# A decoder layer on one core: a new order for all five attention queues, and the gate product read from PSUM

## What is computed

```python
x = x + cross_attention(layernorm(x), ctx, mask)      # 16 heads of 16, rotary, softmax over 256 keys
x = x + gated_linear_attention(layernorm(x))          # 16 heads, decayed state, per-head norm,
                                                      # silu(inputs @ Wg + bg) * o @ Wo
x = x + ffn(layernorm(x))                             # shared expert + top 2 of 7 routed experts
```

## Time and profile before

| | before |
|---|---|
| median of 3 runs | 1606.47 us (1604.30 to 1606.73) |
| the profiled execution, its own time | 1609.45 us |
| its span, first to last instruction | 1607.6 us |
| TensorE busy, whole span | 1451.6 us (90%) |
| VectorE, ScalarE, GpSimd busy | 1097.7, 855.7, 775.0 us |
| chain that ended last, by engine | TensorE 56%, VectorE 23%, ScalarE 11%, DMA 4% |
| first product of keys | at 30.21 us |
| first product of the experts | at 939.15 us |

### The profile page before, as it was taken

One profiled execution on the slowest core, in us unless ns is written; L12 is line 12 of the kernel. 1 busy time (PEld: TensorE's weight loads), 2 busy tenths in 40 slices (PEclk: granted clock), 3 DMA queues, 4 the chain that ended last, 5 costly groups with the idle time before them and its releaser, 6 DMA issues.

```text
span 1607.6 us, 43463 instructions
## 1 busy us (share of the span) xinstructions
PE 1451.6 (90%) x17222; PEld 1090.2 (68%) x17222; DVE 1097.7 (68%) x1975; ACT 855.7 (53%) x1850; POOL 775.0 (48%) x689
## 2 busy tenths in 40 slices
PE   3788998999999999999998766999999999999987
PEld 2455665666666766666666555878888888888865
DVE  2786889888888888888888469774444444444457
ACT  1566876777778777777777322452323222222321
POOL 1575777767676767776776300003333333333210
PEclk9898999999999999999999678999999999999998
DMA  5577776777777776767784332643322222222182
GB/s 135 110 161 132 141 135 129 138 143 130 144 129 148 137 149 135 147 129 139 128 154 84 70 99 73 172 138 67 70 69 73 70 71 70 73 71 72 50 265 73
DMA packets 468338, 185.98 MB, mean 116 GB/s; under 512 B 418065, under 2 KB 456289, under 8 KB 468145
## 3 DMA queue, kind: packets, MB, share of 16 engines
q1 hardware_dynamic: 457392, 150.04, 47.2%
q0 software_dynamic: 10752, 33.17, 6.0%
HBM read 62.56 MB, written 18.35 MB: 50 GB/s over the span
## 4 chain that ended last, share of the span: by engine, by line
PE 56%; DVE 23%; ACT 11%; DMA 4%; issue 4%; SPq 2%; POOL 1%; DVEq 0%; POOLq 0%
PE ps L1013 23%; PE ps L1040 11%; PE ps L741 8%; DVE experts L1380 6%; ACT experts L1116 4%; DVE work L1511 4%; PE ps L733 4%; ACT experts L1103 3%; PE ps L758 2%; DVE experts L1468 2%; DMA experts<-experts 2%; PE ps L785 2%; PE ps L728 1%; DVE experts L1419 1%; PE ps L1045 1%
## 5 line engine op out<-in xcount | busy, mean ns | idle before, releaser
L1013 PE MATMUL ps<-work,experts 128*128 128x256 f16 x3564 | 408.3, 276 | 36.9 <-DVE work L1675 13.9
L1013 PEld LDWEIGHTS ps<-work,experts 128*128 (+1 forms) x3564 | 344.8, 99 | 91.3 <-DVE work L1675 14.7
L741 PE MATMUL ps<-experts 128*128 128x512 f16 (+2 forms) x2304 | 364.9, 310 | 30.9 <-DVE work L1524 14.5
L741 PEld LDWEIGHTS ps<-experts 128*128 128x128 f16 x2304 | 198.9, 100 | 174.1 <-DVE work L1524 28.7
L1103 ACT ACTIVATE work<-work 128x768 f16<-128x768 f32 (+1 forms) x140 | 104.4, 745 | 379.0 <-PE ps L1045 245.1
L1116 ACT ACTIVATE experts<-ps,experts 128x256 f32<-128x256 f32 x512 | 203.3, 473 | 74.9 <-DVE experts L1380 74.7
L687 POOL DMA_INDIRECT work<-token_in,work x76 | 73.8, 971 | 317.3 <-DMA work<-work 225.8
L620 POOL TENSOR_TENSOR experts<-experts 128x1024 f16<-128x1024 f32 x96 | 191.8, 1998 | 59.8 <-ACT experts L1103 59.8
L1040 PE MATMUL ps<-experts,work 128*128 (+1 forms) x1620 | 198.3, 276 | 3.7 <-DVE work L1688 3.7
L1040 PEld LDWEIGHTS ps<-experts,work 128*128 128x128 f16 x1620 | 155.5, 99 | 29.5 <-DVE work L1688 4.1
L1380 DVE TENSOR_REDUCE experts<-ps 128x4 f32<-128x1024 f32 x128 | 155.8, 1218 | 11.6 <-PE ps L758 10.5
(11 more groups left out here) (193 smaller groups left out, 2188.8 us busy)
## 6 DMA issues: line engine op xcount, KB each, us to landing
experts<-in_ctx SPq DMA_DIRECT2D x32, 512.0 KB, 5.0
experts<-choice_out POOLq DMA_DIRECT2D x8, 1024.0 KB, 13.1
experts<-in_x SPq DMA_DIRECT2D x32, 128.0 KB, 2.3
token_in<-experts SPq DMA_DIRECT2D x32, 128.0 KB, 2.8
work<-in_L_ffn_routed_gate SPq DMA_DIRECT2D x8, 352.0 KB, 3.1
experts<-experts SPq DMA_TRANSPOSE x160, 4.6
work<-in_L_ffn_routed_up SPq DMA_DIRECT2D x8, 320.0 KB, 4.2
out<-x_all POOLq DMA_DIRECT2D x5, 512.0 KB, 3.3
```

Source lines behind the costliest of these rows:

```text
L741: ins = pe.matmul(bank, lhs[a][k], rhs[b][k], start=(k == 0 and a + b == 0), stop=(last and k == len(lhs[0]) - 1 and a == 1))
L1013: ins = pe.matmul(out, experts_h[:, e, lo:lo + P], e_rows_t[k][:, b * DK + kk, :], start=(kk == 0 and a + b == 0), stop=(kk == DK - 1 and ...
```

## The change

All five `step(s)` functions get another order and other lags, with the waits that belong to them; `STEPS` goes from 41 to 40. Several products write other PSUM banks. Three things are more than order:

- `g_copy` is gone from ScalarE, and `g_gated` reads the product of `weigh_g` in PSUM.
- The three products with weights ahead of the steps move into steps 0 and 1 of TensorE and VectorE (`start_turn`, `start_bias`, `start_weight`, `start_split`).
- ScalarE splits the shared expert after step 5 instead of 4 (`SHARED_HIGH`).

```diff
-        def g_copy(p):
-            copy(g_out, ps[:, 6, 0:D], S["g_copy_done"])
         def g_gated(p):
-            dve.wait_ge(S["gate_silu_done"], p + 1)
-            dve.wait_ge(S["g_copy_done"], p + 1)
-            v.tensor_tensor(g_out, g_out, gate_i, ALU.mult).then_inc(S["g_gated_done"], 1)
+            v.tensor_tensor(g_out, ps[:, 6, 0:D], gate_i, ALU.mult).then_inc(S["g_gated_done"], 1)
...
         def turn_ctx(p):
             sp.wait_ge(S["ctx_low_done"], p + 1)
-            wait(sp, S["proj_v1_done"], p)
+            if 1 <= p <= 2:
+                wait(sp, S["proj_v_done"], 2 * p)
...
+            at(s, 0, start_turn, 0, 1)
...
+            at(s, 0, start_weight, 0, 1)
...
+            at(s, 2, start_split, 0, 1)
...
+            at(s, 1, start_bias, 0, 1)
...
-STEPS = NPAIR + 9
+STEPS = NPAIR + 8
 SPLIT_STEP = 3
-SHARED_HIGH = 4
+SHARED_HIGH = 5
```

More of the change, by code:

```diff
@@ L375, in program, with at @@
     choices = choice_out[0:TOPK * NTILE * P, :].rearrange("(c p t) d -> p c t d", c=TOPK, p=P)
-    def at(s, lag, op, first=0):
-        if first <= s - lag < NPAIR:
+    def at(s, lag, op, first=0, last=NPAIR):
+        if first <= s - lag < last:
             op(s - lag)
@@ L949, in g_proj @@
             pe.wait_ge(S["gn_copy_done"], p + 1)
[L950 removed]
+            if p == 30:
+                pe.wait_ge(S["gate_silu_done"], p + 2)
+            product(ps[:, 4, 0:D], [g_norm_t[:, k, :] for k in range(DK)], [w_go[:, k, :] for k in range(DK)], S["g_proj_done"])
         def turn_x2n(p):
             pe.wait_ge(S["x2_norm_done"], p + 1)
[L954 to L955 removed]
@@ new lines, in start_turn, with start_weight @@
+        def start_turn(p):
+            pe.wait_ge(S["start_loaded"], 16 * START_DMAS)
+            pe.wait_ge(S["start_ready"], 7)
+            for k in range(DK):
+                pe.transpose(ps[0:16, 7, k * P:(k + 1) * P], w_g1[:, k, :], ident)
+            product(ps[:, 7, D:2 * D], [bv_rows[:, a, :] for a in range(2)], [w_o[:, a, :] for a in range(2)], S["start_mm"])
+        def start_weight(p):
+            pe.wait_ge(S["start_ready"], 8)
+            for k in range(DK):
+                ins = pe.matmul(ps[:, 0, k * P:(k + 1) * P], w_g1_t[0:16, k, :], w_g2[0:16, :], start=True, stop=True)
+            ins.then_inc(S["start_mm"], 1)
@@ L981, in step @@
-            at(s, 2, turn_heads1)
-            at(s, 0, proj_q)
+            at(s, 0, turn_xn)
+            at(s, 1, turn_q)
+            at(s, 3, g_scores)
+            at(s, 0, proj_q)
+            at(s, 0, start_turn, 0, 1)
+            at(s, 2, weigh0)
+            at(s, 1, scores0)
+            at(s, 2, turn_heads0)
+            at(s, 6, turn_x2n)
+            at(s, 2, weigh1)
+            at(s, 3, weigh_g)
+            at(s, 2, turn_heads1)
+            at(s, 4, g_proj)
             at(s, 2, proj_out)
-            at(s, 3, weigh_g)
@@ L992, in _ @@
         pe.wait_ge(S["consts_loaded"], 16)
-        pe.wait_ge(S["start_loaded"], 16 * START_DMAS)
-        for k in range(DK):
-            ins = pe.transpose(ps[0:16, 0, k * P:(k + 1) * P], w_g1[:, k, :], ident)
-        ins.then_inc(S["start_mm"], 1)
-        pe.wait_ge(S["start_ready"], 7)
-        product(ps[:, 2, 0:D], [bv_rows[:, a, :] for a in range(2)], [w_o[:, a, :] for a in range(2)], S["start_mm"])
-        pe.wait_ge(S["start_ready"], 8)
-        for k in range(DK):
-            ins = pe.matmul(ps[:, 1, k * P:(k + 1) * P], w_g1_t[0:16, k, :], w_g2[0:16, :], start=True, stop=True)
@@ L1002, in _ @@
-        ins.then_inc(S["start_mm"], 1)
-        pe.wait_ge(S["start_ready"], 11)
         pe.wait_ge(S["fill_ready"], 1)
@@ L1585, in x1_norm, with start_bias, start_split @@
             v.tensor_scalar(x1n, x1[p % 2], stats[1][:, 6:7], stats[1][:, 9:10], ALU.subtract, ALU.mult).then_inc(S["x1_norm_done"], 1)
-        def step(s):
+        def start_bias(p):
+            dve.wait_ge(S["start_mm"], 1)
+            dve.wait_ge(S["start_loaded"], 16 * START_DMAS)
+            v.tensor_copy(w_g1_t[0:16], ps[0:16, 7, 0:DK * P].rearrange("p (k n) -> p k n", k=DK))
+            v.tensor_tensor(b_o, ps[:, 7, D:2 * D], b_o, ALU.add).then_inc(S["start_ready"], 1)
+        def start_split(p):
+            w_kg = ps[:, 0, 0:DK * P].rearrange("p (k n) -> p k n", k=DK)
+            v.tensor_scalar(w_kg_s[0], w_kg, W_SCALE, None, ALU.mult).then_inc(S["start_ready"], 1)
+            dve.wait_ge(S["start_ready"], 9)
+            v.scalar_tensor_tensor(out=w_kg_s[1], in0=w_kg, scalar=W_SCALE, in1=w_kg_s[0], op0=ALU.mult, op1=ALU.subtract)\
+                .then_inc(S["start_ready"], 1)
+        def step(s):
+            at(s, 2, k_sin0)
+            at(s, 2, k_cos0)
+            at(s, 4, decay_abs)
+            at(s, 2, k_sin1)
+            at(s, 5, g_normed)
+            at(s, 4, log_decay)
+            at(s, 2, v_lo0)
+            at(s, 2, k_cos1)
+            at(s, 6, x2_stats)
+            at(s, 4, g_queries)
+            at(s, 2, v_lo1)
+            at(s, 2, start_split, 0, 1)
+            at(s, 4, g_keys)
             at(s, 4, g_mask1)
```

403 lines of the change are left out of this document (177 added, 226 removed).

## The result

| | before | after |
|---|---|---|
| median of 5 runs each | 1606.47 us (1603.24 to 1609.95) | 1616.27 us (1613.14 to 1617.81) |
| ratio | | 1.0056, 95% interval 1.0038 to 1.0073 |
| profiled execution, span | 1607.6 us | 1615.7 us |
| granted clock of TensorE, mean of the span | 0.966 | 0.944 |
| pair 2's to pair 28's `weigh_g`, 26 steps | 688.12 us, 26.47 a step | 689.81 us, 26.53 a step |

The changed kernel is 9.8 us slower, 0.6%; the forecast was 16 us faster, and the time lies 1 us above the top of its range, 1615. By parts of the span, after against before: 3.4 us more until pair 2's `weigh_g` (167.06 against 163.66), 1.7 in the 26 steps, 6.8 from there to the experts (94.12 against 87.37), and 3.7 less in the experts, whose code is the same. The sum is the 8.1 us between the spans. The forecast had -4, -12, 0 and 0.

What follows compares the result with a forecast made beforehand. A loop over SP's queue and the DMA was taken to bound a step. 26 steps at -0.47 us gave -12, the start -4, the end 0: 1606.47 - 16 = 1590 us, range 1562 to 1615.

Steps and rivals of the forecast that it cites:

- The loop: From weigh1 through proj_out, x1n_low and SP's transposes back to weigh1: bounds a step, 25.7 us in the new order.
- (a): On TensorE from weigh1 to its proj_out, with weigh_g, turn_heads1 and g_proj between: 4.3 us against 3.6.
- (b): From proj_out to the end of x1n_low: 4.9 us against 5.07.
- (d): In SP's queue, turn_x1n and load_pad with two gaps until the first of four transposes is issued: 2.4 us.
- (e): From the issue of the first of the four transposes to its landing: 4.6 us.
- (f): Landings of the three further transposes, one behind another, 3.1 us apart: 9.3 to 9.5 us.
- rival 2: The four transposes in a row stretch, landing 3.5 us apart: loop 27.1 us a step, 1627 us in all; chance 0.16.
- rival 1: Transposes follow faster, from 2.6 us apart on: the step falls to about 24.6 us, 1560 us in all; chance 0.2.
- The start: Ahead of the steps: first keys near 23.5, 6.7 us earlier; 4 us of gain taken because VectorE's weight split intervenes.
- The end: End of the attention, pair 31's chain with lags of 6 instead of 5 for the logits: 0, 3 us either way.
- Rival 3: x1_norm on VectorE waits for GpSimd's p_lo01, 0.4 us a step on the loop: 1600 us; chance 0.14.
- The gate product: g_gated on VectorE, 2076 ns to about 0.43 us: nothing by itself, but lets VectorE keep up in the new order.

Runs made afterwards that it cites:

- e3: Changed kernel with load_pad moved in SP's queue from ahead of the four transposes of the probabilities to behind them: 1580.06 us, ratio 0.9827.
- e4: Kernel before with only the gate product changed (g_gated reads PSUM, g_copy gone), all queues as before: 1603.02 us, ratio 0.9989.
- e10: Kernel before with load_pad alone moved in SP's queue behind turn_p11: 1601.47 us, ratio 0.9943.
- e16: Kernel before with two edits, g_gated reading PSUM and load_pad behind turn_p11 in SP's queue: 1590.73 us, ratio 0.9887.
- e13: e3 with the order behind weigh1 changed to g_proj, turn_heads1, weigh_g, proj_out: 1620.99 us, ratio 1.0106.
- e6: e3 with four added matmuls of 128x256 f16 (0.44 us, output overwritten) between weigh1 and weigh_g: 1584.73 us, ratio 0.9854.
- e2: Changed kernel with eight added matmuls of 128x256 f16 (0.9 us, output overwritten) between weigh1 and weigh_g: 1615.85 us, ratio 1.0061.
- e15: Changed kernel with the order behind weigh1 changed to g_proj, turn_heads1, weigh_g, proj_out, no product added: 1627.29 us, ratio 1.0137.
- e14: e13 with VectorE's split of the gla weights laid into three pieces: 1611.09 us, ratio 1.0045.
- e7: e3 with VectorE's split of the gla weights, 8.8 us in one piece, laid into three pieces: 1572.92 us, ratio 0.9788.
- e1: Changed kernel with four added matmuls of 128x512 f16 (0.85 us, output overwritten) ahead of TensorE's wait at weigh1: 1604.89 us, ratio 0.9990.
- e12: e3 with proj_q moved to just ahead of weigh1 and VectorE's split of the gla weights in three pieces: 1614.74 us, ratio 1.0048.
- e5: Changed kernel with the gate product taken back (g_copy behind g_square again, g_gated with both inputs in SBUF): 1615.88 us, ratio 1.0063.

## Why the prediction was wrong

**The loop: right as the bound, 0.7 us too long.** In the second step shown, `weigh1` starts at 540.33, its `proj_out` is half of the eight matmuls, at 544.7: (a) 4.4, I had 4.3. x1n_low ends 4.9 later, (b) as said. (d) is 1.9 instead of 2.4, since `load_pad` took 0.57. The four transposes are issued from 526.69 and the next `weigh1` starts at 540.33: 13.6 for (e) and (f) with (g), 14.1 said. A plain step is 25.0, and I had said 25.7: with that alone the 26 steps would have gained 18 us more than forecast. e3 (the wait nearly gone when 0.68 us leave the loop) confirms that the loop bounds the changed kernel; for the kernel before, e4 (the idle time moves to `weigh1`), e10 and e16 (their intervals exclude no change) do. The first and the last of the four transposes in the step shown, each with its landing:

```profile
L423 SPq DMA_TRANSPOSE experts<-experts x1: 3064/3064/3064, 526.7 to 526.7; - x1
DMA to landing us min/median/max: 5.3/5.3/5.3
L423 SPq DMA_TRANSPOSE experts<-experts x1: 3140/3140/3140, 535.2 to 535.2; - x1
DMA to landing us min/median/max: 5.0/5.0/5.0
```

The first lands at 532.0, the last at 540.2: (e) is 5.3 here, not 4.6, and (f) 8.2, 2.7 apart. Over the 26 steps the first lands 4.5 after its issue and the others 3.0 apart, in the median. So rival 2 is out, the four transposes do not stretch, and so is rival 1, whose pace was 2.6 or less.

**The step that failed: the sum of (a) to (g) took TensorE's work at one pace.** The durations in (a) and (b) came from rows at the full clock. I had seen that the change puts `weigh_g` behind `weigh1`, and priced it at its 2.04 us, but not asked what the stretch does to the clock. It falls in 16 steps, in 15 of them behind these two groups; `g_proj` and `proj_out` stand there, on the loop; each fall adds about 2.0 us. That is 30 us over the 26 steps, a term that the sum did not have. With it taken off they would be 28 us shorter than before, more than the 12 that I forecast. So two errors partly cancelled: the loop at the full clock was put 0.7 us a step too long, and the clock was left out. That the time came out only 1 us above the range is luck.

That the clock falls there, and that this lengthens the loop, is shown by rows. The price of 2.0 us rests on the two estimates, 2.0 and 1.9, and is not the same everywhere: in e13 a step with a fall is only 1.0 us longer than a plain one, and in e6 seven falls less brought no gain. What brings the falls is shown in part. Wide f16 products between the two groups take nearly all of them away, with the order around them kept (3 falls in e2 and in e6, with the clock of every run of e2 above that of every run of the changed kernel, and of e6 above e3). That the direct sequence of the two groups is the cause is not shown: without it e15 has 7, but e13 and e14 have 9 and 8, as many as e3 and e7 with it (10 and 7), and e1 has it and 8 falls. e4 has 13 in the old order, with long waits ahead of `weigh1`. A run of small products can do it with no idle time (the row of e3), and more idle time goes with more falls (e4); what exactly the chip looks at stays open.

**The start: wrong by 7 us.** The keys do start at 24.53, I had said 23.5. But the gain went behind them. One part is the split, which I had seen and priced at 2.7 of 6.7 us: TensorE stands 8.0 us there (e7, e12, e14: 4 to 10 us). Pair 0's `weigh_g` starts at 107.34, 4.6 later than before, pair 2's 3.4 later. The other part is the clock again. From the first keys to pair 2's `weigh_g`, before and after:

```profile
30.21:163.66 133.45, 110.34 (x1294) 0.91 0.64 127
```

```profile
24.53:167.06 142.53, 114.05 (x1282) 0.84 0.65 124
```

TensorE idles 5.4 us more and is busy 3.7 us more, with twelve matmuls fewer, at a mean clock of 0.84 against 0.91. No run separates the two parts.

**The end: wrong by 7 us.** I had put the longer lags at 0, with 3 either way. From pair 28 to the experts it is 6.8 us more:

```profile
851.78:939.15 87.37, 62.20 (x905) 0.75 0.36 73
```

```profile
856.87:950.99 94.12, 69.29 (x925) 0.75 0.37 65
```

TensorE's idle time is the same, 25.2 and 24.8 us; the added time is work, with 20 matmuls more and the same low clock. So waits for the later logits are not it. Part of the 6.8 is where the stretch is cut: in the new order `g_proj` and `proj_out` of a step stand behind its `weigh_g`. The 3.7 us less in the experts have no reason in the code; their mean clock was 0.98 against 0.97.

**Rival 3: the mechanism is real, and small.** In the changed kernel `x1_norm` took 383 ns in the median and 559 at most (min/median/max of its 26):

```profile
L1571 DVE TENSOR_SCALAR work<-work x26: 380/383/559, 174.8 to 837.3; 128x256 f32<-128x256 f32 x26
```

It meets GpSimd's split of the probabilities in 10 of the 26 steps and then takes 0.17 us longer, not 0.4, some 2 us in all. In e5 it meets it in 14, and in 13 of them takes 0.83, until GpSimd is done (at 492.3 in the rows at the end).

**The gate product: right in its cost, wrong in its role.** By itself it is worth nothing measurable (e4), as said. "In the new order it is what lets VectorE keep up" is false (e5).

## What to carry to other kernels

When a loop over several engines bounds a step, list every instruction of every queue on it, small ones above all: here moving a load of 64 KB on SP's queue was worth 36 us in the new order, while the new order as it stood cost 10. Before small matmuls are put one behind another, read the granted clock over the stretch, since a sum of durations taken at the full clock has no term for its fall. And a part of a change that measures nothing alone is not shown to be useless: e4 by itself lies within the noise of the kernel before, while with the load moved the same edit takes the gain from 9 to 18 us (e10, e16), with intervals that just overlap.

## What the runs showed of the hardware that was not expected

- TensorE's clock falls to 1.2 GHz while the engine is busy without a gap: 0.57 from 497 to 501 us in e3_pad_behind, behind 48 matmuls of 33 and 64 of 16 columns, with no idle time ahead. That is 3.4 us at the lower level, as in the changed kernel from 517 on.
- VectorE's `g_gated` with two inputs in SBUF waits for GpSimd's `tensor_tensor` (2076 ns) but not for its `tensor_scalar`: in e5_after_gcopy the two overlap in all 26 steps, and `g_gated` takes 408 to 419 ns. VectorE's `tensor_scalar`, on the other hand, waits for GpSimd's `tensor_tensor`. Both in e5_after_gcopy (timelines of the two engines):

```profile
490.32 2.00 POOL L617 TENSOR_TENSOR experts<-experts 128x1024 f16<-128x1024 f32 x1 [4.44 <-ACT experts L1093]
491.64 0.83 DVE L1577 TENSOR_SCALAR work<-work 128x256 f32<-128x256 f32 x1
...
521.07 1.23 POOL L655 TENSOR_SCALAR experts<-experts 128x256 f32<-128x256 f32 x1
521.95 0.42 DVE L1500 TENSOR_TENSOR work<-work 128x256 f32<-128x256 f32 x1
```

The span of a GpSimd instruction is rough, and the overlap is 0.1 to 0.36 us, so that the two ran side by side is less sure than that 0.42 is the undisturbed time.
- The median from issue to landing of the transposes of the probabilities is longer with four in a row, though their spacing is not. Before and after, from 160 to 860 us:

```profile
DMA to landing us min/median/max: 4.3/4.7/6.9
```

```profile
DMA to landing us min/median/max: 4.3/5.2/7.5
```

The 4.6 of the earlier trace rows also holds the transposes of the context. That each waits for those ahead of it fits, but is not shown.
